# Openings and end of attention rearranged in a one-core Perceiver block: transposes, stores, first keys, x and the order of the output projection

## The reference

```python
q = (scale * (Q @ Wq + bq)).reshape(bs, q_len, NH, DM)     # Q = layernorm(x): 512 x 512, NH = 16, DM = 64
k = (K @ Wk + bk).reshape(bs, kv_len, NH, DM)              # K = V = context: 8192 x 512
v = (V @ Wv + bv).reshape(bs, kv_len, NH, DM)
a = jax.nn.softmax(jnp.einsum('nlhd,nshd->nhls', q, k), axis=-1)
o = jnp.einsum('nhls,nshd->nlhd', a, v).reshape(bs, q_len, NH * DM)
x = x + o @ Wo + bo
...
x = x + _L0_attn_ref(_layernorm(x, axis=-1), ...)
x = x + _L0_ffn_ref(_layernorm(x, axis=-1), ...)
```

## Time and profile before

| | |
|---|---|
| median of 3 runs | 2537.85 us (2537.58 to 2538.69) |
| profiled execution, its own time | 2538.53 us |
| span of its trace | 2536.8 us |
| busy | PE 94%, DVE 78%, ACT 63%, POOL 27% |
| mean granted TensorE clock | 0.978 |
| latent queries | 0 to 43 us |
| keys and values | 43 to 866 us |
| attention | 867 to 1831 us |
| all later stages | 1831 us to the end |

### The profile page before, as it was taken

How to read it: one execution, slowest core, us unless ns; L and a number is a source line. 1 busy time by engine, 2 the same in 40 slices (tenths; PEclk the granted TensorE clock), 3 DMA queues, 4 the chain that set the end, 5 groups by cost and what they waited for, 6 DMA issues and landing times. The chain is left out here.

```text
span 2536.8 us, 39407 instructions
## 1 busy us (share of the span) xinstructions
PE 2396.1 (94%) x14143; PEld 1015.5 (40%) x14143; DVE 1978.6 (78%) x1982; ACT 1605.1 (63%) x1973; POOL 679.0 (27%) x468
## 2 busy tenths in 40 slices
PE   6999999999999799999999999999787778998999
PEld 3333333333333244444444444444332323444554
DVE  5777777777777788888888898888579993267996
ACT  5555555565555477888878787888384441237994
POOL 1455555555555400000000000000029990010001
PEclk9999999999999899999999999999888998999999
DMA  7244654455445592433333342432340005148994
GB/s 249 84 150 156 205 168 149 158 174 165 149 143 154 149 251 76 124 91 103 96 97 102 95 108 77 122 92 87 114 166 1 0 0 199 50 158 327 404 404 174
DMA packets 177959, 366.02 MB, mean 144 GB/s; under 512 B 19490, under 2 KB 90275, under 8 KB 174179
## 3 DMA queue, kind: packets, MB, share of 16 engines
q1 hardware_dynamic: 176290, 360.75, 44.4%
q0 software_dynamic: 1280, 4.20, 0.5%
q10 hardware_dynamic: 322, 0.21, 0.0%
HBM read 254.24 MB, written 106.68 MB: 142 GB/s over the span
## 5 line engine op out<-in xcount | busy, mean ns | idle before, releaser
L452 DVE TENSOR_REDUCE kv_mx<-kv_s 128x1024 f32 (+1 forms) x512 | 595.6, 1218 | 224.8 <-PE kv_s L488 224.8
L795 DVE TENSOR_TENSOR at_pl<-at_pf,at_ph 128x1024 f16<-128x1024 f32 x512 | 613.2, 1223 | 116.0 <-ACT at_ph L742 107.2
L748 ACT ACTIVATE at_pf<-at_st 128x1024 f32<-128x1024 f32 x512 | 497.6, 1025 | 189.2 <-PE at_st L913 184.2
L912 PE MATMUL at_st<-keep_big,at_k_cur 128*128 (+1 forms) x1024 | 391.0, 382 | 11.9 <-DMA at_k_one<-kd 9.6
L913 PE MATMUL at_st<-keep_big,at_k_one 128*128 (+1 forms) x1024 | 389.6, 380 | 0.0
L742 ACT ACTIVATE at_ph<-at_pf 128x1024 f16<-128x1024 f32 x256 | 272.7, 1065 | 0.0
L1107 POOL MEMSET mamba_zero<- 128x2 f32 x1 | 0.1, 100 | 945.9 <-POOLq L60 945.9
L876 PE MATMUL at_acc<-at_ph,at_vs 128*128 128x512 f16 x1024 | 242.6, 379 | 2.7 <-DVE at_pl L795 2.6
L368 POOL TENSOR_TENSOR kv_ksl<-kv_kf,kv_ksh 128x512 f16<-128x512 f32 x128 | 148.1, 1157 | 247.3 <-ACT kv_ksh L396 247.3
L1021 PE MATMUL kv_kp<-first_ch,first_wkh 128*128 128x512 f16 x512 | 195.4, 382 | 5.3 <-DVEq L434 5.3
L393 ACT ACTIVATE kv_kf<-kv_kp,first_bks 128x512 f32<-128x512 f32 x128 | 87.4, 683 | 171.6 <-PE kv_kp L1021 171.6
(11 more groups left out here) (357 smaller groups left out, 3881.2 us busy)
## 6 DMA issues: line engine op xcount, KB each, us to landing
keep_big<-gate_up SPq DMA_DIRECT2D x17, 2048.0 KB, 11.1
at_k_cur<-kd SPq DMA_DIRECT2D x128, 256.0 KB, 3.8
at_vs<-vd SPq DMA_DIRECT2D x64, 512.0 KB, 3.9
vd<-kv_vs SPq DMA_DIRECT2D x15, 2048.0 KB
kv_tf<-wpack SPq DMA_DIRECT2D x21, 1024.0 KB, 9.7
keep_big<-down SPq DMA_DIRECT2D x17, 1024.0 KB
first_cf<-ctxT SPq DMA_DIRECT2D x16, 1024.0 KB, 12.8
at_k_one<-kd SPq DMA_DIRECT2D x64, 256.0 KB, 4.3
```

The costliest lines, as they stand in the source:

```text
L452: nc.vector.reduce_max(mx[:, bass.ds(g * (NH * TT) + 2 * (m - TT), 2)], s1[:, m % 3, :, :], AX.X).then_inc(s1_max, 1)
L748: nc.scalar.activation(pf[:, s % FULL, :, :], st[:, s % HP % NST, :, :], ACT.Exp, scale=SCORE).then_inc(pf_ready, 1)
L795: nc.vector.tensor_tensor(pl[:, s % RING, :, :], pf[:, s % FULL, :, :], ph[:, s % RING, :, :], ALU.subtract).then_inc(pl_ready, 1)
L912: nc.tensor.matmul(st[:, w % NST, e, :], k_cur[:, tile], qh[:, q], start=True, stop=False)
```

## The change

At the opening of the latent queries PE transposes one row tile after the other, each as soon as its xn is there, and the first pair's product waits for the low parts chunk by chunk. DVE scales the query bias behind the low parts. The second pair of query stores goes into the next stage, ahead of SP's first weight loads. At attention's opening the first key quarter is loaded in two pieces, the first of four pairs of key tiles (FK = 1024 columns) on a semaphore of its own; the third query load goes to SP behind it; the row of maxima comes from `mrow` in SBUF. At attention's end x is loaded ahead of the last sums' store, and x + bias is added ahead of the last pair's scaling. The projection takes the first six pairs for all row tiles as before, and the last two pairs tile by tile.

```diff
 WT = TW * (NCK // 2 - 1)
+def store_queries(eng, keep, q_dram, half):
+    js = slice(half * 4, half * 4 + 4)
+    for s, q in enumerate((keep.qh[:, js, :], (keep.ch, keep.cl)[half][1][:, :, :])):
+        eng.dma_start(q_dram[s].rearrange("(j p) t -> p j t", p=P)[:, js, :], q).then_inc(keep.q_out, 16)
...
             load_context(1, next_in)
-            for js, low in ((slice(0, 4), keep.ch[1]), (slice(4, 8), keep.cl[1])):
-                sp.wait_ge(ql_ready, js.stop)
-                for s, q in enumerate((qh[:, js, :], low[:, :, :])):
-                    sp.dma_start(q_dram[s].rearrange("(j p) t -> p j t", p=P)[:, js, :], q).then_inc(keep.q_out, 16)
+            sp.wait_ge(ql_ready, PAIRS // 2)
+            store_queries(sp, keep, q_dram, 0)
             sp.wait_ge(next_in, 16)
...
                                         ALU.subtract, ALU.mult).then_inc(xn_ready, 1)
-            dve.wait_ge(b_in, 16)
-            nc.vector.tensor_scalar(bqs[:, :], bqc[:, :], SA, None, ALU.mult).then_inc(b_ready, 1)
             split(0)
...
                                                ALU.subtract).then_inc(xl_ready, 1)
+            dve.wait_ge(b_in, 16)
+            nc.vector.tensor_scalar(bqs[:, :], bqc[:, :], SA, None, ALU.mult).then_inc(b_ready, 1)
             split(1)
...
             pe.wait_ge(made, 2)
-            pe.wait_ge(xn_ready, TT)
-            transpose_rows(nc, xn, xT, ident, xT_ready)
-            pe.wait_ge(xl_ready, DC)
+            for t in range(TT):
+                pe.wait_ge(xn_ready, t + 1)
+                for c in range(DC):
+                    last = nc.tensor.transpose(xT[:, c, t * P:(t + 1) * P], xn[:, t, c * P:(c + 1) * P], ident[:, :])
+                    if t == TT - 1:
+                        last.then_inc(xT_ready, 1)
             for j in range(PAIRS):
...
                 cols = slice(j * P, (j + 1) * P)
-                product(nc, qp[:, j % 4, :], [p for c in range(DC) for p in
-                                              three(wh[:, c, cols], wl[:, c, cols], xh[:, c, :], xl[:, c, :])]
-                        ).then_inc(q_ready, 1)
+                for c in range(DC):
+                    if j == 0:
+                        pe.wait_ge(xl_ready, c + 1)
+                    last = product(nc, qp[:, j % 4, :],
+                                   three(wh[:, c, cols], wl[:, c, cols], xh[:, c, :], xl[:, c, :]),
+                                   start=(c == 0), stop=(c == DC - 1))
+                last.then_inc(q_ready, 1)
...
+            store_queries(sp, keep, q_dram, 1)
             for e in range(TW):
...
-        def load_queries(eng, first, end, sem):
+        Q_PARTS = ((qh, 0, 0), (ql, 1, 0), (qh, 0, DH))
+        FK = SP * 2 * P
+        def load_queries(eng, first, end, sem, which=Q_PARTS):
             src = q_dram.rearrange("s (h d) t -> s d h t", d=DH)
-            for q, s, at in ((qh, 0, 0), (ql, 1, 0), (qh, 0, DH)):
+            for q, s, at in which:
                 eng.dma_start(q[at:at + DH, first * T:end * T].rearrange("d (h t) -> d h t", t=T),
...
         def _(sp):
-            def load_keys(n, q):
-                cols = slice(q * QK, (q + 1) * QK)
+            def load_keys(n, q, first=0, end=QK, sem=None):
+                cols = slice(q * QK + first, q * QK + end)
                 for k, s, at in ((k_cur, 0, 0), (k_cur, 1, DH), (k_one, 0, 0)):
                     sp.dma_start(k[at:at + DH, cols],
-                                 kd[s].rearrange("d h n -> d (h n)")[:, bass.ds(n * S + q * QK, QK)]).then_inc(k_in[q], 16)
+                                 kd[s].rearrange("d h n -> d (h n)")[:, bass.ds(n * S + q * QK + first, end - first)]
+                                 ).then_inc(sem or k_in[q], 16)
             def load_values(n, q):
...
                              .rearrange("p h s -> p (h s)")).then_inc(v_in[q], 16)
-            for q in range(NQ):
+            load_keys(0, 0, 0, FK, k_first)
+            load_queries(sp, 0, 1, q_in, Q_PARTS[2:])
+            load_keys(0, 0, FK)
+            load_values(0, 0)
+            for q in range(1, NQ):
                 load_keys(0, q)
...
             load_split(sp, wsplit, W.O, k_cur[:, 0:2 * WC], k_one[:, 0:2 * WC], w_in)
+            sp.wait_ge(pl_ready, NH * HP + RING)
+            sp.dma_start(xs, x.rearrange("(t p) d -> p t d", p=P)).then_inc(small_in, 16)
             store(PAIRS - 1, 1)
             factors(PAIRS - 1)
-            sp.wait_ge(pl_ready, NH * HP + RING)
-            sp.dma_start(xs, x.rearrange("(t p) d -> p t d", p=P)).then_inc(small_in, 16)
             sp.wait_ge(st_ready, NH * HP)
...
-            load_queries(act, 0, 1, q_in)
+            load_queries(act, 0, 1, q_in, Q_PARTS[:2])
             act.wait_ge(ql_zero, 1)
-            act.wait_ge(m_out, 16)
-            act.dma_start(ql[DH:DH + 1, 0:T], m_dram[0:T].rearrange("(o n) -> o n", o=1)).then_inc(q_in, 16)
+            act.dma_start(ql[DH:DH + 1, 0:T], mrow[0:TT, :]).then_inc(q_in, 16)
             pair_turns(act, pair, lambda h: None, {HIGH_AT: high}, lambda: act.wait_ge(consts, 2))
...
             reciprocals(PAIRS - 1)
+            dve.wait_ge(small_in, 32)
+            for t in range(TT):
+                nc.vector.tensor_tensor(xs[:, t, :], xs[:, t, :], bob, ALU.add).then_inc(xs_ready, 1)
             scale(PAIRS - 1)
             low(PAIRS - 1)
             own.n = 4 * PAIRS
-            dve.wait_ge(small_in, 32)
-            for t in range(TT):
-                own.inc(nc.vector.tensor_tensor(xs[:, t, :], xs[:, t, :], bob, ALU.add))
-            own.wait()
+            dve.wait_ge(xs_ready, TT)
             for t in range(TT):
...
                     pe.wait_ge(q_rest_in, 64)
-                if w % QP == 0:
+                if isinstance(g, int) and g == 0:
+                    pe.wait_ge(k_first, 48)
+                elif w % QP == 0 or w == SP:
                     pe.wait_ge(k_in[w // QP], 48 * (h + ahead + 1))
...
             pe.wait_ge(w_in, 32)
-            for j in range(PAIRS):
+            LATE = PAIRS - 2
+            for j, t in [(j, t) for j in range(LATE) for t in range(TT)] + [
+                    (j, t) for t in range(TT) for j in range(LATE, PAIRS)]:
                 pe.wait_ge(ol_ready, j + 1)
-                for t in range(TT):
-                    tok = slice(t * P, (t + 1) * P)
-                    last = product(nc, yp[t], three(oh[:, j, tok], ol[:, j, tok], woh[:, j, :], wol[:, j, :]),
-                                   start=(j == 0), stop=(j == PAIRS - 1))
-                    if j == PAIRS - 1:
-                        last.then_inc(y_ready, 1)
+                tok = slice(t * P, (t + 1) * P)
+                last = product(nc, yp[t], three(oh[:, j, tok], ol[:, j, tok], woh[:, j, :], wol[:, j, :]),
+                               start=(j == 0), stop=(j == PAIRS - 1))
+                if j == PAIRS - 1:
+                    last.then_inc(y_ready, 1)
             pe.wait_ge(made, 2)
```

12 lines of the change are left out of this document (6 added, 6 removed).

## The result

The changed kernel takes 2530.82 us (median of 9 runs, 2528.3 to 2533.05) against 2537.85 us (9 runs, 2536.89 to 2539.63): ratio 0.9967, 95% interval 0.9959 to 0.9976. So it is faster, by 7.0 and 6.5 us between the medians, 8.4 and 5.8 us by the ratios; forecast were 6.15 us. The profiled execution took 2530.96 us, its span 2529.1 us (before 2536.8 us).

The account below looks back on a forecast made before the run. PE, busy in nearly every slice, was taken as the bound, so only its waits counted. Terms −1.35 (latent queries and stores), −1.8 and −3.0 sum to −6.15 us: 2537.85 becomes 2531.7 us, range 2529.5 to 2534.4 us.

Parts of the forecast that it names:

- Latent queries, opening: Latent queries: tile-by-tile transposes let ACT's second weight split start earlier, −0.25 us; PE's earlier first product counted as nothing.
- Moved stores: Barrier into the key/value stage: it waits for DVE instead of SP's second pair of query stores, −1.1 us.
- rival 3: Key/value stage: moved query stores land late and hold ACT's write of ch1, +1.45 us in all, 2539.3 us; chance 0.04.
- Attention's opening: Attention's start: smaller key loads start PE about 2.2 us sooner, part lost to GpSimd memsets, −1.8 us (bounds 0 to −2.75).
- rival 1: Attention's opening gives almost nothing, 0.5 us, as loads, row or memsets hold PE; sum −4.85 us, 2533.0 us; chance 0.22.
- Two arrivals at once: Attention's opening: keys and row of maxima arrive within 0.1 us of each other, so shortening one alone would bring nothing.
- Attention's end: Attention's end: early x and last two pairs projected tile by tile let DVE finish at 1818.5 instead of 1821.53 us, −3.0 us.
- rival 2: Key/value stage: PE starts sooner and full clock may return earlier; 2 us less half speed gives −1.0 us, 2530.6 us; chance 0.12.
- a sign of being wrong: Later stages, which the change doesn't touch: the prediction would be wrong if they took a different time than before.

Follow-up runs that it names:

- warm: Kernel before plus extra identity products on PE around its transposes in the latent queries' opening; 2537.04 us against 2539.18, ratio 0.9993.
- p_store: Kernel before with only the second pair of query stores moved into the next stage; its time is not told from no change.
- before_a: The kernel before, unchanged, run once more for its profile; 2543.72 us in one run.
- before_relief: Kernel before with two of GpSimd's last fills in attention's opening done by DVE at the stage's start; 2537.44 us against 2539.43, ratio 0.9991.
- o_keys: Kernel before with only the key pieces and the third query load on SP, row still through m_dram; 2541.06 us against 2537.32, one run.
- before_b: The kernel before, unchanged, run a second further time for its profile; 2536.78 us in one run.
- fill: Changed kernel plus 13 extra PE products in the gap ahead of the key/value stage; 2529.79 us, ratio 0.9967 to the kernel before.
- both: Changed kernel with fill's products, two GpSimd fills moved to DVE, and 9 zero products before PE's query wait; 2528.81 us, ratio 0.9964.
- both_b: Same kernel as both, timed on another chip beside the changed kernel; 2528.91 us, ratio 0.9964 to the kernel before.

## Why the prediction was right in direction and short in size

Two steps failed: PE's earlier first product in the latent queries, counted as nothing, was worth 0.92 us on average, and the term of attention's opening was 0.86 us too small. The mechanisms of the stores and of the end were as forecast.

- **Latent queries, opening, −0.25 us: too small; the step that failed most.** The text said of PE's earlier first product: "I count nothing for it, since DVE's chain, not PE, ends the stage." That is so in the trace that I read, in which all products ran at full speed; from the first xn to the last low part the changed kernel's profile takes 31.35 us against its 31.65 us, 0.30 us less. In 8 of 11 traces with the old opening half-speed products made PE the one that DVE waits for. Between the means of the table the last low part ends 42.22 − 40.52 = 1.70 us sooner (seven new traces). Of this 0.45 us lies ahead of the first xn (9.49 and 9.04 us), where no edit stands; warm, with the old opening, has 9.04 us too. The stretch behind it is 1.26 us shorter: 0.92 us are those waits (12.57 to 11.65), which I had counted as nothing, and 0.34 us the chain from the first xn to the key bias, for which I had 0.25.
- **Moved stores, −1.1 us: right.** 2.34 to 1.25 us in p_store and in the changed kernel. The second landed 4.8 us after its issue at 41.90 us (4.5 at its old place), and ACT wrote ch1 from 50.09 us, straight behind its other work: rival 3 didn't come.
- **Attention's opening, −1.8 us: measured −2.66 us, and by another mechanism.** This is the second term that was mis-sized. PE starts 2.45 us sooner, near the 2.2 forecast. But what I took off for memsets isn't a share. In the kernel before the first CAST is held until 15.83 us behind the barrier by the memset from 13.48 to 15.28 us, and everything behind it is pinned: PE may start at 6.70 or 7.88 us, the values come at 20.24 us. In the changed kernel the first CAST slips in ahead and the second is held, to 16.27 us. That is one period of DVE won (18.14 to 21.24 us before, 3.10 us) less 0.44 us: 2.66 us. A start 0.39 us sooner (before_a) was worth nothing; rival 1 was nearer than its text knew. before_relief shows the pin itself: with the last fills taken from GpSimd, and PE starting at 6.86 us, the opening is 1.63 us shorter. The rule cited in the prediction from the Trainium skill ("SBUF — State Buffer", "SBUF: two separate sides") goes with these rows: a CAST that meets a memset ends 0.55 us behind it in all of them, and takes 0.7 to 0.8 us otherwise. DVE's subtraction for pl isn't held: 1.22 or 1.23 us beside a memset and without, before and after the change. Rival 1's lesser saving, 0.9 us in place of 1.8, makes the sum −5.25 us, just outside the 0.2% (5.1 us) and not within it as its text has it; the k_one load of half the size landed 2.7 us sooner, at 2.8 instead of 5.5 us.
- **Two arrivals at once: wrong in a detail.** "shortening one alone would bring nothing": the keys and the query load on SP, without the row, brought it all (o_keys).
- **Attention's end, −3.0 us: 3.28 us between the two profiles, right.** Over ten traces with the old end and seven with the new the means are 30.30 and 27.59 us, −2.71 us; the spread, 1.5 us on either side, comes with the DMAs of the sums.
- **The clock (rival 2): it was there, not as put.** The key/value stage was 1.2 us shorter in the changed kernel's profile (819.13 for 820.36 us), but the earlier start isn't the reason: over all traces the stage takes 819.4 us with the old opening and 819.6 us with the new. Only a filled gap takes the slow stretch away.
- **The sum.** The segments' means give −1.26 − 1.10 − 2.66 − 2.71 = −7.7 us; the two ratios give −8.4 and −5.8 us with intervals of some 2 us to either side, so the whole times bear out both 7.7 and 6.15 us. What is shown, by the segments and not by the times, is that the terms of the two openings were too small by 1.0 and 0.86 us; that of the end was 0.3 us too large. From the transposes to the end of the span the changed kernel's profile takes 712.8 us, 1.4 more than before (711.4), for which the prediction had no term but a sign of being wrong. The unchanged kernel's own three profiles take 711.4, 711.6 and 714.3 us there, the changed kernel's two 712.8 and 713.2, so chance alone makes such differences; whether the change adds to it is open. Some 1 us of it falls in the first 50 us, of which the half level takes 11.3 and 11.4 us in the changed kernel's two profiles, 6.1 and 6.4 us in before and before_b, but 11.9 us in before_a.

## What to carry to other kernels

One trace is one draw: a term costed at nothing because an engine "isn't what the stage ends with" should be asked for again with that engine at half its clock, and a second profile of the unchanged kernel costs less than a wrong sum. Look in an opening for work of fixed start (fills on another engine) that can pin it; then gains come in steps of the pipeline's period, or not at all, whatever is saved ahead of it. Two edits at one place (x early, tile order) can be worth half and nothing alone, so try them together before one is dropped.

## What was not expected of the hardware

- A 128 KB load of k_one landed 2.8 us after its issue, the 256 KB one 5.5 us: nearly in proportion to bytes, with the loads issued ahead of it halved as well.
- A GpSimd memset can be held as well: 2.23 us instead of 1.80 when DVE's CAST ran as it began (875.22 and 875.51 us above).
- PE standing 3.4 to 7.4 us ahead of the key/value stage brought the half level in that stage in all 16 traces, until 2.7 to 5.9 us behind its first product; 1.2 to 1.5 us of standing brought none (fill, both, both_b).
- The clock column can read 1.00 where the profile holds no clock level: before_a's slow products show in their durations alone (0.63 us for 0.38).
